# A perceiver's first cross-attention in float16 pairs, keys placed by transfers, transposes among key products, chunks unrolled

## The chip, the cores and the metric

The kernel runs on one core of one Trainium2 chip. The metric is the device time of one execution in microseconds (us), the median of several runs. A core has TensorE (PE; PEld is its weight load), VectorE (DVE), ScalarE (ACT), GpSimd (POOL) and SyncE (SP), which here only issues transfers. The engines run side by side and wait for each other through semaphores. ps is PSUM, the eight accumulation banks.

## The reference

Two perceiver layers on a latent x of 128 x 256 with a context of 12544 x 256: cross-attention, self-attention and a feed-forward part, each behind a layer norm and added to x. Only the first cross-attention is touched:

```python
def _L0_xattn_ref(x, context, ln_gamma, ln_beta, w_q, w_kv, w_out, b_out, gate):
    xn = _layernorm(x, ln_gamma, ln_beta)
    q = (xn @ w_q).reshape(B, SQ, 16, 64)
    k, v = jnp.split(context @ w_kv, 2, axis=-1)        # 12544 x 1024 each
    k = k.reshape(B, SK, 16, 64)
    v = v.reshape(B, SK, 16, 64)
    scores = jnp.einsum('bqhd,bkhd->bhqk', q * 64 ** -0.5, k)
    attn = jax.nn.softmax(scores, axis=-1)
    out = jnp.einsum('bhqk,bkhd->bqhd', attn, v).reshape(B, SQ, 1024)
    return (out @ w_out + b_out) * jnp.tanh(gate[0])
x = x + _L0_xattn_ref(_layernorm(x), ctx_1024, ...)
```

## The kernel before

first_cross_attention walks the context in 14 chunks of 896 keys (CH; 7 tiles of 128) and in each chunk over 16 heads: 224 steps, n = 16 c + h. It is an attention with a running row maximum and a rescaled accumulator. Float32 accuracy is had by splitting each operand into a high and a low part and adding three products (high by high, high by low, low by high); for context, weights, keys and queries the parts are float32r, for values and probabilities float16.

A step n does, by engine and line:

- TensorE: scores of step n+1 (L696, four products of 448 columns: q_hi and q_lo, each over two halves of the keys, into the two banks s_scores; the query of a head is there twice, on partitions 0 to 63 and 64 to 127, and meets the key's high part on one half and its low part on the other); the key product of step n+4 (K_AHEAD; L686, six products of 448, one half of the keys of two heads, into the bank s_k); a value product (L663, six products of 512 columns, one tile of 128 keys by 8 heads, bank s_v) at h = 1 to 7 for this chunk's heads 8 to 15 and at h = 9 to 15 for the next chunk's heads 0 to 7; weighing of step n-1 (L705 to L707, 21 products of 64 or 65 columns); seven float32 transposes of the probabilities (L715).
- ACT: copies the key product out (L440 k_raw) and writes the even head's high half to k_st (L441), then the exponential of step n+1 (L432), v_hi (L424), and the two pT_hi from the transposed banks (L485, L487); decay at every fourth head (L481).
- VectorE: drop at every fourth head (L604), the two pT_lo of step n-1 (L553), the row maximum of the scores n+1 (L545) and neg_max with it (L547), the flush of a group of four heads to acc (L560, L563), c_abs of the next chunk at h = 2 and 4 (L526), v_lo (L538) or, at h = 8, the value scale (L532, L534).
- GpSimd: k_split, three operations of 64 x 448 on float32r, which finish k_st (L363, L367, L370), each behind a semaphore of the one before; at h < 8 one of eight pieces of the next chunk's c_hi and c_lo (L352, L355); the rescaling of acc at every fourth head (L386).
- SP: one load of the next chunk into c_raw per chunk (L324).

k_st holds two head pairs. Each engine runs its list in order. Scores of a step wait for the exponential of the step before, since s_scores is single. Chunks 0 and 1 and chunks 12 and 13 are written out straight; chunks 2 to 11 are a loop of five passes of two chunks, on each engine:

```python
def chunk_pairs(engine, two_chunks):
    two_chunks(0, True, False)
    with engine.Fori(1, NCH // 2 - 1) as i:
        two_chunks(i * 2, False, False)
    two_chunks(NCH - 2, False, True)
```

Before the steps stands a head: layer norm, weight splits, query product and its doubling, the first four key products and the first seven value tiles. The weights of the later ternary feed-forward part are loaded, summed and quantised inside chunks 0, 1, 12 and 13.

## Time and profile before

| | |
|---|---|
| median of 3 runs | 1608.9 us (1608.52 to 1609.34) |
| profiled execution, first to last instruction | 1607.9 us |
| instructions | 30564 |
| busy: PE, PEld | 86%, 71% |
| busy: DVE, ACT, POOL | 66%, 54%, 58% |
| first cross-attention, first to last exponential | 40.0 to 1200.9 us |
| GpSimd's k_split (L363, L367, L370) | 207.3, 250.9, 253.9 us busy |
| row maximum (L545) | 241.7 us busy, 224 times |

The busy share is an average over stages. A row of a group gives the line, the engine, what is written from what with shapes, how often, the busy time, the mean of one instruction, and how long the engine idled before it and for whom. A row of a timeline gives start, duration, engine, line, operation and, in brackets, the idle time before it; "x7" means seven merged. The records of TensorE's products overlap, since they are pipelined: the spacing of their starts is what one costs. "issue" is a wait for nothing that the profile shows.

### The profile page before, as it was taken

The page shows a single profiled execution, that of the slowest core. Times are in us where ns is not written, and L with a number is a line of the kernel's source. Part 1 is how long each engine was busy: PE and PEld are TensorE (multiplying, and loading weights), DVE is VectorE, ACT ScalarE, POOL GpSimd, SP SyncE. Part 2 cuts the span into 40 slices and gives each one's busy share as a digit, 9 for nine tenths or more (in the row PEclk, how much of TensorE's full clock was granted, in tenths as well). Part 3 has the DMA queues.
Part 4 walks back from the last instruction along what each step waited for, and adds up shares of the span by engine and source line. Part 5 has one row for each costly group of instructions (what it writes and reads, how often), then busy time and mean ns, then how long its engine had stood idle before and what let it go on. Part 6 is the DMA issues. An engine that isn't in the chain of part 4 may idle for free. (4 is left out here: it accounts for less than half of the span.)

```text
span 1607.9 us, 30564 instructions
## 1 busy us (share of the span) xinstructions
PE 1379.2 (86%) x10913; PEld 1137.1 (71%) x10913; DVE 1054.0 (66%) x1695; ACT 860.9 (54%) x1614; POOL 926.3 (58%) x850
## 2 busy tenths in 40 slices
PE   5999999998999899989998999999974689515498
PEld 3788888887888788878887788888863348402288
DVE  6677676766777677757676667777753461499732
ACT  4676666665666566656666566678651013154010
POOL 2778777876777686858686778787750000056300
PEclk9999999999999999999999999999997699757789
DMA  6000000000000000000000000000006347030145
GB/s 252 1 24 1 24 1 24 1 24 3 24 2 24 3 24 1 24 3 11 14 4 23 2 24 2 24 1 2 1 27 220 91 166 226 35 151 1 38 178 199
DMA packets 38529, 76.61 MB, mean 48 GB/s; under 512 B 3472, under 2 KB 26832, under 8 KB 38112
## 3 DMA queue, kind: packets, MB, share of 16 engines
q1 hardware_dynamic: 37552, 71.37, 13.1%
q10 hardware_dynamic: 816, 3.15, 0.5%
q8 instruction: 95, 1.56, 0.4%
q14 instruction: 66, 0.54, 0.1%
HBM read 74.34 MB, written 0.16 MB: 46 GB/s over the span
## 5 line engine op out<-in xcount | busy, mean ns | idle before, releaser
L363 POOL TENSOR_TENSOR k_st<-k_raw,one 64x448 fp32r<-64x448 f32 x220 | 207.3, 942 | 248.7 <-ACT k_raw L440 245.9
L538 DVE SCALAR_TENSOR_TENSOR v_lo<-ps,v_scale,v_hi 128x512 f16<-128x512 f32 x196 | 147.0, 751 | 271.9 <-ACT v_hi L424 271.9
L553 DVE TENSOR_TENSOR pT_lo<-ps,pT_hi 128x512 f16<-128x512 f32 x448 | 256.9, 614 | 70.0 <-ACT pT_hi L485 60.4
L432 ACT ACTIVATE p_exp<-ps,neg_max 128x896 f32<-128x896 f32 x224 | 224.7, 1003 | 113.4 <-DVE neg_max L547 112.7
L367 POOL TENSOR_TENSOR k_st<-k_raw,k_st 64x448 fp32r<-64x448 f32 x220 | 250.9, 1141 | 31.5
L440 ACT ACTIVATE k_raw<-ps 128x448 f32<-128x448 f32 x220 | 120.0, 545 | 277.7 <-PE ps L686 277.5
L370 POOL TENSOR_TENSOR k_st<-k_raw,k_st 64x448 fp32r<-64x448 f32 x220 | 253.9, 1154 | 17.3
L545 DVE TENSOR_REDUCE neg_row<-ps 128x1 f32<-128x896 f32 x224 | 241.7, 1079 | 7.1 <-PE ps L696 7.1
L715 PE MATMUL ps<-ident,p_exp 128*128 128x128 f32 x1568 | 217.5, 279 | 0.0
L696 PE MATMUL ps<-k_st,q_hi 128*128 128x448 f32 x448 | 144.6, 404 | 52.8 <-ACT p_exp L432 30.7
L705 PEld LDWEIGHTS ps<-v_hi,pT_hi 128*128 128x128 f16 x1568 | 142.8, 99 | 65.4 <-issue 53.6
L705 PE MATMUL ps<-v_hi,pT_hi 128*128 128x65 f16 x1568 | 169.2, 196 | 5.8 <-DVE pT_lo L553 5.4
L715 PEld LDWEIGHTS ps<-ident,p_exp 128*128 128x128 f32 x1568 | 170.4, 142 | 0.1
L686 PE MATMUL ps<-c_hi,wk_hi 128*128 128x448 f32 x448 | 167.5, 374 | 3.0 <-DVE k_st L588 3.0
L686 PE MATMUL ps<-c_lo,wk_hi 128*128 128x448 f32 x448 | 167.5, 374 | 0.0
L686 PE MATMUL ps<-c_hi,wk_lo 128*128 128x448 f32 x448 | 167.3, 374 | 0.0
L706 PE MATMUL ps<-v_lo,pT_hi 128*128 128x64 f16 x1568 | 167.1, 194 | 0.0
L707 PE MATMUL ps<-v_hi,pT_lo 128*128 128x65 f16 x1568 | 166.3, 194 | 0.0
L663 PE MATMUL ps<-wv_hi,c_hi 128*128 128x512 f32 x392 | 154.4, 394 | 1.0 <-DVE v_lo L538 1.0
L663 PE MATMUL ps<-wv_hi,c_lo 128*128 128x512 f32 x392 | 154.7, 395 | 0.0
L663 PE MATMUL ps<-wv_lo,c_hi 128*128 128x512 f32 x392 | 154.3, 394 | 0.0
L706 PEld LDWEIGHTS ps<-v_lo,pT_hi 128*128 128x128 f16 x1568 | 144.8, 98 | 0.0
(304 smaller groups left out, 2682.0 us busy)
## 6 DMA issues: line engine op xcount, KB each, us to landing
c_raw<-in_ctxT SPq DMA_DIRECT2D x14, 896.0 KB, 4.7
xa_ct<-in_ctxT SPq DMA_DIRECT2D x14, 896.0 KB, 4.7
xa_cn<-in_ctx SPq DMA_DIRECT2D x14, 896.0 KB, 5.2
me_w<-in_me_w SPq DMA_DIRECT2D x8, 1536.0 KB, 7.7
me_w<-in_me_w SPq DMA_DIRECT2D x8, 768.0 KB, 4.7
ss_b_all<-ss_bc SPq DMA_DIRECT2D x1, 2048.0 KB, 6.8
ss_c_all<-ss_bc SPq DMA_DIRECT2D x1, 2048.0 KB, 11.4
wk<-in_wk ACTq DMA_DIRECT2D x1, 1024.0 KB, 5.4
```

What stands on the lines that cost most here:

```text
L363: nc.gpsimd.tensor_tensor(k_st[DH:P, tile, 1, keys], k_raw[DH:P, u % 2, :], one[DH:P, 0, :].to_broadcast([DH, HCH]), ALU.mult).then_inc(k_ ...
L367: nc.gpsimd.tensor_tensor(k_st[DH:P, tile, 0, keys], k_raw[0:DH, u % 2, :], k_st[0:DH, tile, 0, keys].bitcast(F32), ALU.subtract).then_inc ...
L370: nc.gpsimd.tensor_tensor(k_st[0:DH, tile, 1, keys], k_raw[DH:P, u % 2, :], k_st[DH:P, tile, 1, keys].bitcast(F32), ALU.subtract).then_inc ...
L432: nc.scalar.activation(p_exp[:, h % 2, :].rearrange("p (b k) -> p b k", b=2), s_scores, ACT.Exp, bias=neg_max[:, par, h:h + 1]).then_inc(e ...
L545: nc.vector.tensor_reduce(neg_row[:, h % 2:h % 2 + 1], s_scores, AX.XY, ALU.max, negate=True).then_inc(row_max_done, 1)
L553: nc.vector.tensor_tensor(pT_lo[:, h % 2, t0:t1, :], s_t[b][:, 0:(t1 - t0) * S].rearrange("p (t s) -> p t s", s=S), pT_hi[:, h % 2, t0:t1, ...
L663: mm = nc.tensor.matmul(v_bank(use, early), lhs, rhs, start=(k == 0), stop=(k == 5))
L686: mm = nc.tensor.matmul(k_bank(u, early), lhs, rhs, start=(k == 0), stop=(k == 5))
L705: nc.tensor.matmul(s_pv[h // 4 % 2][:, h % 4, :], ph, v_hi[:, tile, h, 0:DH + 1], start=(tile == 0), stop=False)
L706: nc.tensor.matmul(s_pv[h // 4 % 2][:, h % 4, 0:DH], ph, v_lo[:, tile, h, 0:DH], start=False, stop=False)
L707: mm = nc.tensor.matmul(s_pv[h // 4 % 2][:, h % 4, :], pl, v_hi[:, tile, h, 0:DH + 1], start=False, stop=(tile == TILES - 1))
L715: mm = nc.tensor.transpose(s_t[b][:, s * S:(s + 1) * S], p_exp[:, h % 2, tile * P:(tile + 1) * P], ident[:, :])
```

## The change

- All parts are float16. So that they fit, context, weights and query are scaled first: by the largest weight of each input row (w_abs, w_inv) and a bound per chunk (w_bound times c_abs on TensorE, then un, c_scale), the query by q_scale; the exponential takes the inverse as scale (esc), and the new neg_new applies it to the row maximum. v_lo no longer scales and is a tensor_tensor.
- The key product is copied by ACT as before (k_raw), then GpSimd makes k_top (float16 copy, 128 x 448) and k_rest (the remainder), two operations in place of three, and SP places their halves into k_st by four transfers a step. k_st has four pairs, K_AHEAD is 6. The first six key products go by ACT and VectorE.
- TensorE's step: scores n+1, then transposes of step n alternating with the six products of key n+6, then weighing n-1, then the value product, which waits for v_lo of the one before (v_ready).
- VectorE's step: drop, row_max n+1 (three operations), v_lo, first pT_lo, flush, c_abs at h = 2, 3, scale at h = 4, second pT_lo. ACT's step: v_hi, first pT_hi, exponential n+1, second pT_hi, key copy, at h = 6 to 9 c_hi, at every fourth decay.
- GpSimd's step: c_low at h = 7 to 10, c_times at h = 5 to 8 (scaling in place), acc's rescaling at every fourth, k_split.
- No loop; all 14 chunks are written out. The ternary quantisation goes over chunks 2 to 7.

```diff
-K_AHEAD = 4
+K_AHEAD = 6
-        k_st = t("k_st", [P, 2, 2, CH], F32R)
+        k_st = t("k_st", [P, 4, 2, CH], F16)
+        k_top, k_rest = t("k_top", [P, 2, HCH], F16), t("k_rest", [P, 2, HCH], F16)
...
@@ SP @@
+                for n in range(NT):
+                    U = n + K_AHEAD
+                    if U < NT:
+                        b = U % 2
+                        at_least(sp, scores_done, 2 * (U // 2 - 4) + 2)
+                        sp.wait_ge(k_top_ready, U - K_AHEAD + 1)
+                        for side in range(2):
+                            r = DH * side
+                            sp.dma_start(k_st[(slice(r, r + DH),) + k_place(U, side)], k_top[r:r + DH, b, :]).then_inc(k_placed[b], 16)
+                        sp.wait_ge(k_rest_ready, U - K_AHEAD + 1)
+                        for side in range(2):
+                            r, other = DH * side, DH * (1 - side)
+                            sp.dma_start(k_st[(slice(other, other + DH),) + k_place(U, side)], k_rest[r:r + DH, b, :]).then_inc(k_placed[b], 16)
...
@@ GpSimd @@
+                def k_split(U):
+                    i, b = U - K_AHEAD, U % 2
+                    pool.wait_ge(k_raw_ready, i + 1)
+                    if i >= 2:
+                        pool.wait_ge(k_placed[b], k_turn(U - 2))
+                    nc.gpsimd.tensor_copy(k_top[:, b, :], k_raw[:, b, :]).then_inc(k_top_ready, 1)
+                    pool.wait_ge(k_top_ready, i + 1)
+                    nc.gpsimd.tensor_tensor(k_rest[:, b, :], k_raw[:, b, :], k_top[:, b, :], ALU.subtract).then_inc(k_rest_ready, 1)
...
@@ ACT @@
+                for n in range(NT):
+                    c, h = n // H0, n % H0
+                    if n and v_at(n - 1):
+                        v_high(*v_at(n - 1))
+                    at_least(act, pv_done, n - 1)
+                    act.wait_ge(t0_done, n + 1)
+                    turned(n, 0)
+                    if n + 1 < NT:
+                        exponent(n + 1)
+                    act.wait_ge(t1_done, n + 1)
+                    turned(n, 1)
+                    if n + K_AHEAD < NT:
+                        k_copy(n + K_AHEAD)
...
@@ VectorE @@
+                def row_max(n):
+                    v.wait_ge(scores_done, n + 1)
+                    link(nc.vector.tensor_reduce(neg_row[:, i:i + 1], s_scores, AX.XY, ALU.max, negate=True))
+                    link(nc.vector.tensor_scalar(neg_new[:, i:i + 1], neg_row[:, i:i + 1], esc[:, par:par + 1], LN_K, ALU.mult, ALU.add))
+                    nc.vector.tensor_tensor(neg_max[:, par, h:h + 1], neg_new[:, i:i + 1], neg_max[:, 1 - par, h:h + 1],
+                                            ALU.min).then_inc(neg_max_ready, 1)
...
@@ TensorE @@
+                for n in range(NT):
+                    if n + 1 < NT:
+                        scores(n + 1)
...
+                    if U < NT:
+                        k_wait(U)
+                    for tile in range(TILES):
+                        turn(n, tile)
+                        if U < NT and tile < 6:
+                            k_part(U, tile)
...
+                    if n:
+                        weigh(n - 1)
+                    if v_at(n):
+                        v_project(*v_at(n))
```

## Rows read from the trace of the kernel before

**Rows 1.** Windows view, steady stretch: busy us per engine, clock, DMA share, GB/s
```profile
650.00:697.00 47.00, 44.99 (x397) 38.38 (x397) 33.42 (x55) 30.36 (x55) 36.24 (x35) 1.00 0.06 21
```

**Rows 2.** Source view of the exponential's line: durations in ns, first and last start
```profile
L432 ACT ACTIVATE p_exp<-ps,neg_max x224: 992/1007/1011, 40.0 to 1200.9; 128x896 f32<-128x896 f32 x112
```

**Rows 3.** Timeline, ACT, chunk starts: start us, duration, operation, idle before
```profile
797.68 1.01 ACT L432 ACTIVATE p_exp<-ps,neg_max 128x896 f32<-128x896 f32 x1 [0.70 <-DVE neg_max L547]
...
880.18 1.01 ACT L432 ACTIVATE p_exp<-ps,neg_max 128x896 f32<-128x896 f32 x1 [0.70 <-DVE neg_max L547]
...
891.29 0.99 ACT L432 ACTIVATE p_exp<-ps,neg_max 128x896 f32<-128x896 f32 x1
```

**Rows 4.** Timeline, TensorE, at the start of a loop pass
```profile
713.51 0.64 PE L696 MATMUL ps<-k_st,q_hi 128*128 128x448 f32 x2 [2.81 <-issue]
```

**Rows 5.** Timeline of all engines but TensorE's, one step
```profile
652.60 1.01 ACT L432 ACTIVATE p_exp<-ps,neg_max 128x896 f32<-128x896 f32 x1 [0.70 <-DVE neg_max L547]
...
654.22 0.75 DVE L538 SCALAR_TENSOR_TENSOR v_lo<-ps,v_scale,v_hi 128x512 f16<-128x512 f32 x1 [0.66 <-ACT v_hi L424]
...
655.95 1.08 DVE L545 TENSOR_REDUCE neg_row<-ps 128x1 f32<-128x896 f32 x1
...
656.85 0.93 POOL L363 TENSOR_TENSOR k_st<-k_raw,one 64x448 fp32r<-64x448 f32 x1 [0.54 <-ACT k_raw L440]
...
657.07 0.73 DVE L547 SCALAR_TENSOR_TENSOR neg_max<-neg_row,neg_max 128x1 f32<-128x1 f32 x1
...
657.83 1.01 ACT L432 ACTIVATE p_exp<-ps,neg_max 128x896 f32<-128x896 f32 x1 [0.70 <-DVE neg_max L547]
...
657.92 1.14 POOL L367 TENSOR_TENSOR k_st<-k_raw,k_st 64x448 fp32r<-64x448 f32 x1
```

**Rows 6.** Timeline, TensorE, one step
```profile
652.05 0.20 PE L705 MATMUL ps<-v_hi,pT_hi 128*128 128x65 f16 x1
...
652.69 0.96 PE L715 MATMUL ps<-ident,p_exp 128*128 128x128 f32 x7
653.76 0.64 PE L696 MATMUL ps<-k_st,q_hi 128*128 128x448 f32 x2
...
654.64 0.37 PE L686 MATMUL ps<-c_hi,wk_hi 128*128 128x448 f32 x1
...
655.88 0.39 PE L663 MATMUL ps<-wv_hi,c_hi 128*128 128x512 f32 x1
...
657.03 0.40 PE L663 MATMUL ps<-wv_hi,c_lo 128*128 128x512 f32 x1
```

**Rows 7.** Source view of neg_max: minimum, median, maximum in ns
```profile
L547 DVE SCALAR_TENSOR_TENSOR neg_max<-neg_row,neg_max x224: 158/604/942, 39.8 to 1200.7; 128x1 f32<-128x1 f32 x112
```

**Rows 8.** Groups of VectorE by shape, 300 to 1100 us: busy us, mean ns, idle
```profile
L553 DVE TENSOR_TENSOR pT_lo<-ps,pT_hi 128x512 f16<-128x512 f32 x152 | 103.6, 682 | 44.5 <-ACT pT_hi L485 35.0 <-issue 9.5
...
L617 DVE TENSOR_SCALAR wq<-wq 128x1024 f32<-128x1024 f32 x2 | 2.1, 1056 | 0.0
L534 DVE RECIPROCAL v_scale<-v_unscale 128x1 f32<-128x1 f32 x10 | 1.6, 164 | 0.3
```

**Rows 9.** Groups of TensorE's weight loads by shape, up to 1240 us
```profile
L715 PEld LDWEIGHTS ps<-ident,p_exp 128*128 128x128 f32 x1568 | 170.4, 142 | 0.1
...
L705 PEld LDWEIGHTS ps<-v_hi,pT_hi 128*128 128x128 f16 x1568 | 142.8, 99 | 65.4 <-issue 53.6 <-DVE pT_lo L553 9.8 <-DVE acc L563 1.9
```

**Rows 10.** DMA issues up to 60 us: KB each, median us from issue to landing
```profile
c_raw<-in_ctxT SPq DMA_DIRECT2D x2, 896.0 KB, 10.7
...
x<-in_x SPq DMA_DIRECT2D x1, 128.0 KB, 2.8
```

**Rows 11.** Timeline, head: transfer issue, c_abs, score product of step 1
```profile
2.21 0.63 SPq L297 DMA_DIRECT2D rows<-in_rows  x1
...
13.89 2.08 DVE L526 TENSOR_REDUCE c_abs<-c_raw 128x1 f32<-128x896 f32 x2 [0.56 <-DMA c_raw<-in_ctxT]
...
45.33 0.57 PE L696 MATMUL ps<-k_st,q_hi 128*128 128x448 f32 x2
```

More of the change, by code:

```diff
@@ L399, in _, with c_times, c_low @@
-                chunk_pairs(pool, two_chunks)
+                def c_times(c, k):
+                    par = c % 2
+                    pool.wait_ge(c_scale_ready, c + 1)
+                    nc.gpsimd.tensor_scalar(c_raw[raw_part(k)], c_raw[raw_part(k)], c_scale[:, par, k % 2:k % 2 + 1], None,
+                                            ALU.mult).then_inc(c_scaled, 1)
+                def c_low(c, k):
+                    par = c % 2
+                    pool.wait_ge(c_hi_ready, 4 * c + k + 1)
+                    nc.gpsimd.tensor_tensor(c_lo[c_part(par, k)], c_raw[raw_part(k)], c_hi[c_part(par, k)], ALU.subtract).then_inc(c_lo_ready, 1)
@@ new lines, in _ @@
+                for k in range(4):
+                    c_times(0, k)
+                for k in range(4):
+                    c_low(0, k)
+                pool.wait_ge(ones_ready, 5)
+                for n in range(NT):
+                    c, h = n // H0, n % H0
+                    if 7 <= h <= 10 and c + 1 < NCH:
+                        c_low(c + 1, h - 7)
+                    if 5 <= h <= 8 and c + 1 < NCH:
+                        c_times(c + 1, h - 5)
+                    if h % 4 == 3:
+                        g = h // 4
+                        f = c * 4 + g
+                        pool.wait_ge(decay_ready, f + 1)
+                        at_least(pool, flushed, 2 * (f - 3))
+                        grp = acc[:, 4 * g:4 * g + 4, :]
+                        nc.gpsimd.tensor_tensor(grp, grp, decay[:, 4 * g:4 * g + 4].unsqueeze(2).to_broadcast([P, 4, DH + 1]),
+                                                ALU.mult).then_inc(acc_scaled, 1)
+                    if n + K_AHEAD < NT:
+                        k_split(n + K_AHEAD)
@@ new lines, in _, with c_high @@
+                act.wait_ge(w_scale_ready, 2)
+                for c in range(DC):
+                    nc.scalar.activation(wk_hi[:, c, :], wk[:, c, :], ACT.Copy, scale=w_inv[:, c:c + 1]).then_inc(wk_hi_ready, 1)
+                def c_high(c, k):
+                    par = c % 2
+                    act.wait_ge(c_scaled, 4 * c + k + 1)
+                    if c >= 2:
+                        act.wait_ge(k_written, 16 * (c - 1))
+                        act.wait_ge(v_written, 14 * (c - 1))
+                    nc.scalar.activation(c_hi[c_part(par, k)], c_raw[raw_part(k)], ACT.Copy).then_inc(c_hi_ready, 1)
@@ new lines, in _, with v_high @@
+                for k in range(4):
+                    c_high(0, k)
+                act.wait_ge(loaded["wv"], 16)
+                for c in range(DC):
+                    nc.scalar.activation(wv_hi[:, c, :], wv[:, c, :], ACT.Copy, scale=w_inv[:, c:c + 1]).then_inc(wv_hi_ready, 1)
+                def v_high(vn, c, half, tile):
+                    act.wait_ge(v_written, vn + 1)
+                    if tile == 0:
+                        at_least(act, pv_done, c * H0 - (8 if half == 0 else 0))
@@ L690, in scores, with bound, k_wait @@
-                def scores(n, h):
-                    pe.wait_ge(k_ready, n * 2 + (4 if h % 2 == 0 else 2))
+                    mm.then_inc(v_written, 1)
+                def bound(c):
+                    pe.wait_ge(absmax_done, 2 * c + 2)
+                    for d in range(DC):
+                        mm = nc.tensor.matmul(s_bound, w_bound[:, d, :], c_abs[:, c % 2, d:d + 1], start=(d == 0), stop=(d == DC - 1))
+                    mm.then_inc(bound_done, 1)
+                def k_wait(U):
+                    c, u = U // H0, U % H0
+                    if U < K_AHEAD:
+                        at_least(pe, k_early, 2 * (U - 2) + 2)
+                    elif U == K_AHEAD:
+                        pe.wait_ge(k_early, 2 * K_AHEAD)
+                    else:
+                        pe.wait_ge(k_raw_ready, U - K_AHEAD)
+                    if u < 2:
+                        pe.wait_ge(c_lo_ready, 4 * c + 2 + 2 * u)
@@ new lines, in k_part @@
+                def k_part(U, k):
+                    c, u = U // H0, U % H0
+                    d, term, b = k // 3, k % 3, u % 2
+                    m = slice(u // 2 * P, (u // 2 + 1) * P)
+                    keys = slice(b * HCH, (b + 1) * HCH)
+                    lhs = (wk_hi, wk_hi, wk_lo)[term][:, d, m]
+                    rhs = (c_hi, c_lo, c_hi)[term][:, c % 2, d, keys]
+                    mm = nc.tensor.matmul(k_bank(U), lhs, rhs, start=(k == 0), stop=(k == 5))
+                    if k == 5:
+                        mm.then_inc(k_written, 1)
```

677 lines of the change are left out of this document (301 added, 376 removed).

## The prediction

> **What bounds the kernel now.** I read first the windows of the steady stretch of the first cross-attention, then its exponentials in order of time, then all engines inside one step, then the rows that price single instructions. In the window TensorE is busy 45.0 of 47 us, VectorE 33.4, ACT 30.4, GpSimd 36.2 [rows 1], so the stage looks bound by TensorE. It isn't, quite. There is one exponential (L432) per step of chunk and head, 224 of them, from 40.0 to 1200.9 [rows 2]: 1160.9 us of the 1607.9, 5.2 a step. The rest of the kernel I take as untouched. Chunk 9 takes 82.5 us (797.68 to 880.18), but the next interval alone is 11.1 us (880.18 to 891.29) [rows 3]. It opens a pass of the loop, and TensorE stands still there, for 2.8 us at one place, waiting for nothing that the trace shows [rows 4]. Four passes show it, at 5 to 6 us each, 22.8 us in all; the straight chunks 0, 1, 12 and 13 don't.
>
> Inside a pass the cadence is 5.23 us (exponentials at 652.60 and 657.83 [rows 5]), while TensorE needs 0.88 for scores, 1.24 for keys, 1.40 for values, 0.64 for weighing and 0.7 for transposes [rows 6], 4.9 in all. What closes the step is a ring of ACT and VectorE: the exponential ends, v_hi follows on ACT, v_lo on VectorE starts at 654.22, then two pT_lo, the row maximum at 655.95, neg_max at 657.07, the next exponential at 657.83 [rows 5]. In it neg_max, a 128x1 operation, takes 0.73 us and ends when GpSimd's k_st copy ends (656.85 + 0.93 = 657.78 [rows 5]). Over all steps it takes 158 ns at least and 604 at the median [rows 7]: this operation has two SBUF inputs and waits out whatever GpSimd runs.
>
> **The change part by part.** The new order makes other rings. I count from a step's first score product.
>
> *Ring with values (14 of 16 steps).* Four score products: three spacings of 0.19 (below) and one record of 0.37 [rows 6] make 0.94. The row maximum is now first in VectorE's step, no longer behind v_lo and pT_lo: 0.03 + 1.08 [rows 5], to 2.05. Then a new small tensor_scalar. Its bounds are 0.16, VectorE's reciprocal [rows 8], and 0.60, neg_max's median [rows 7]; as it reads one tensor like the reciprocal, I take 0.19 with its semaphore. neg_max at its free 0.16 [rows 7]: 2.45. v_lo, now a plain tensor_tensor from PSUM, costs what pT_lo of that shape does, 0.68 [rows 8]: 3.13. The next value product waits for it (one bank), and with it the next scores, queued behind on TensorE. 0.04, then six products of 512 columns in float16. Spacing today is 0.23 for 512 and 0.207 for 448 columns of float32r, 0.0305 for 65 of float16 [rows 6], which is 2.4 GHz in both with some 19 and 3 ns beside: so 0.217 and 0.19. Six make 1.30, the step **4.45 us**.
>
> *TensorE alone.* Scores 0.76, transposes between key products, weighing 0.64, values 1.30. Now a transpose costs 0.11 ((0.96 - 0.27) / 6 [rows 6]), nearer to its weight load of 0.142 [rows 9] than to its 128 columns at 2.4 GHz (0.055). Beside a key product that load is covered: a pair 0.19 + 0.055, six pairs and one transpose 1.6. With nothing gained it is 6 x 0.30 + 0.11 = 1.9. Weighing ends at 3.0 to 3.3, beside the 3.17 at which v_lo frees the bank: float16 and the alternation save TensorE 0.3 to 0.6 us a step, of which almost nothing is on the ring, and cost it 0.1 at most. Loads that are not covered are a rival.
>
> *Ring without values (heads 0 and 8).* Scores to exponential to scores: 2.45 + 0.04 + 1.01 [rows 5] + 0.15 = **3.65**.
>
> *ACT.* Today 30.4 of 47 us [rows 1], 3.4 a step. The half-wide copy into k_st goes (0.5), c_hi comes (four a chunk, 0.5 each). Both stand behind the key copy, where ACT waits for the next value product; 3.0 of 4.45, hidden.
>
> *VectorE.* 1.08 + 0.19 + 0.16 + 0.68 + 0.68 + 0.55 and some 0.4 for flush, c_abs and scales: 3.7 of 4.45. The last pT_lo ends at 4.6, the next maximum is due at 5.4; without that cover each tenth would be on the ring. The ternary quantisation (1.06 [rows 8] and one more operation in chunks 2 to 7) fits but for some 0.5 us.
>
> *GpSimd.* Three key operations of 0.93, 1.14 and one more like it [rows 5] become a one-input copy and a subtraction of 1.15. The copy's bounds are 0.93, today's two-input form, and half of it; I take 0.6. They start after the previous step's key copy, at 0.1, and end at 1.9 (2.25 by the upper bound), before neg_max at 2.28. So most collisions of today go. They stay where GpSimd's queue is longer: behind acc's rescaling (0.6, heads 0, 4, 8, 12) until 2.75, at heads 5 to 10 for c_times (0.6) and c_low (1.15), both from 1.95, and after each short step. Per chunk 4 x 0.45 + 2 x 0.27 + 4 x 0.8 and some 0.5: 6 us.
>
> *Transfers.* Each step issues four from SP, 56 KB each. An issue takes 0.63 in the row [rows 11], at most 2.5 of SP's 4.45; a load of 128 KB lands 2.8 us after its issue [rows 10]. From key copy to landed keys: 0.6 + 1.15 + 1.2 + 2.8, 5.8 us. k_top's buffer is asked for again after two steps, 8.9 us, the keys after four. Hidden with 3 us to spare. Queued behind the waits on SP is c_raw's load at head 11, needed six heads later.
>
> *Chunk.* 14 x 4.45 + 2 x 3.65 + 6 = **75.6 us** against 82.5. Unrolling takes the 22.8 us of the passes; the straight chunks of today are the evidence. Thirteen chunks make 983, the last (seven steps with values, eight without, 2 of collisions) 62.5: 1045 against 1161, so 116 less.
>
> *Head.* c_raw lands at 13.9, the first score of step 1 leaves at 45.3 [rows 11]. Now scales come first: two maxima of 1.04, two of the 2048-wide weights of 2.4 by the same rate, small ones, to 22; four c_times and four c_low on GpSimd to 29; then on VectorE twelve early key subtractions at 0.6, four q_lo at 0.6 and two wv_lo at 1.2, to 42, and seven value tiles at 1.35, the last of them to 50. That is 5 us more, 12 at worst.
>
> Sum: 1607.9 - 116 + 8 (head 5, 3 for the quantisation, the flush after it and the order at the end) = 1500 as the span. The runs' median is 1.0 above the span: **1501 us**.
>
> **Rivals.** (1) *Collisions in every step.* If the copy takes over 0.93, or the new tensor_scalar waits for GpSimd too, each of the two small operations pays today's median excess (0.60 - 0.16) or less, 0.3: 0.6 a step with values in place of the 6 counted gives 79.5 a chunk, 1501 + 54 = 1555. Against it: the reciprocal took 164 ns in ten of ten beside a busy GpSimd, and a tensor_scalar of 1024 elements 1056 ns, one element a cycle [rows 8]. Of its chance of 0.19, 0.08 is for the tensor_scalar. The Trainium skill (SBUF — State Buffer, "Who interferes with whom") says that tensor_scalar can enter a two-port mode and is then locked out by GpSimd. By that rule this rival is the forecast; the rows on the reciprocal and the 1024-wide operation show neither the mode nor a wait. (2) *No collisions.* The phases settle so that GpSimd is free at each neg_max: 69.6 a chunk, 1501 - 80 = 1420. For it: today's minimum of 158 ns. (3) *Slower: weight loads uncovered.* If each load between a float32 transpose and a float16 product stood alone (0.142 and 0.099 [rows 9]), the pairs would take 7 x 0.2 + 6 x 0.29 = 3.1 and the step 0.76 + 3.1 + 0.64 + 1.30 = 5.8: 1501 + 196 x 1.35 - 20 = 1745. It turns into a loss from 5.0 a step. Against it: loads of 0.099 vanish in spacings of 0.0305 today [rows 6, 9]. (4) *Slower: late landing.* The loop of k_top is (0.93 + 1.15 + 0.3 + 1.2 + L) / 2 a step. With L at 2.8 it is 3.2, it binds from L = 5.3 and passes today's 5.2 from 6.8; the nearest row so long is c_raw's 10.7 in the crowded start [rows 10]. With L at 7.5: some 1650. (5) *It doesn't do what it says* in one part: float16 brings no faster stream, since float32r has 2.4 GHz already; this is in the sum.
>
> **How the numbers follow.** Forecast 0.61 (own range 1455 to 1540), every-step collisions 0.19, none 0.12, uncovered loads 0.04, late landing 0.03, all cancelled to within 0.2% 0.01. A measurement of this kernel can tell about 0.2%, 3 us. Faster 0.92, same 0.01, slower 0.07. The range reaches both collision cases: 1425 to 1562.
>
> **What would show it.** Exponentials 4.45 apart with values, 3.65 without, 75.6 a chunk, none 11 apart. The value product idles until v_lo. neg_max mostly at 0.16, long at heads 4 to 10. Scores never wait for transfers. The copy on GpSimd under 0.93. Step 1 starts at 50. It is wrong if TensorE spaces a pair over 0.3, if transfers land after 5 us, or if VectorE has no gap before the maximum. The granted clock should stay at 1.00, 2.4 GHz, as with 45 of 47 us busy [rows 1].

## The result and the profile after

The changed kernel takes **1469.6 us** (median of 4 runs, 1467.7 to 1470.1) against 1608.7 of the kernel before on the same chip: a ratio of 0.9132, 95% interval 0.9119 to 0.9145, so 139 us less. The forecast was 1501 in a range of 1425 to 1562. The profiled span is 1467.4 us. The page of the profile after, with columns as in [rows 8] (busy us, mean ns, idle time before):

```profile
PE 1273.5 (87%) x10912; PEld 894.1 (61%) x10913; DVE 1039.5 (71%) x1976; ACT 798.2 (54%) x1453; POOL 577.3 (39%) x632
...
L350 POOL TENSOR_TENSOR k_rest<-k_raw,k_top 128x448 f16<-128x448 f32 x218 | 226.1, 1037 | 17.7
...
k_st<-k_top SPq DMA_DIRECT2D x436, 56.0 KB, 2.0
```

GpSimd's share fell from 58% to 39%. Two groups of VectorE stand where [rows 7] stood:

```profile
L534 DVE TENSOR_TENSOR neg_max<-neg_new,neg_max 128x1 f32<-128x1 f32 x224 | 50.1, 224 | 7.6
L533 DVE TENSOR_SCALAR neg_new<-neg_row,esc 128x1 f32<-128x1 f32 x224 | 48.0, 214 | 7.9
```

neg_max now takes 224 ns on average, against a median of 604 [rows 7], and the new small tensor_scalar takes 0.21 us in every one of its 224 records. The answer to [rows 5, 6] is one step in order of time (start, duration, engine, line, and in brackets the idle time before and what ended it):

```profile
694.59 0.54 PE L707 MATMUL ps<-k_st,q_hi 128*128 128x448 f16 x2
...
695.35 0.27 PE L717 MATMUL ps<-ident,p_exp 128*128 128x128 f32 x1
695.46 0.35 PE L693 MATMUL ps<-c_hi,wk_hi 128*128 128x448 f16 x1
...
695.55 1.09 DVE L532 TENSOR_REDUCE neg_row<-ps 128x1 f32<-128x896 f32 x1 [0.94 <-PE ps L707]
695.65 0.27 PE L717 MATMUL ps<-ident,p_exp 128*128 128x128 f32 x1
...
696.92 0.16 DVE L534 TENSOR_TENSOR neg_max<-neg_new,neg_max 128x1 f32<-128x1 f32 x1
697.00 0.68 DVE L525 TENSOR_TENSOR v_lo<-ps,v_hi 128x512 f16<-128x512 f32 x1
...
697.12 1.10 ACT L420 ACTIVATE p_exp<-ps,neg_max,esc 128x896 f32<-128x896 f32 x1
...
697.25 0.19 PE L733 MATMUL ps<-v_hi,pT_hi 128*128 128x65 f16 x1
...
697.88 0.38 PE L665 MATMUL ps<-wv_hi,c_hi 128*128 128x512 f16 x1
...
699.17 0.35 PE L707 MATMUL ps<-k_st,q_hi 128*128 128x448 f16 x1
```

The step lasts 699.17 - 694.59 = 4.58 us, and no TensorE row of it carries a wait. A transpose is followed by its key product 0.11 later, and that by the next transpose 0.19 later: a pair is 0.30. The values start at 697.88, 3.29 into the step, when v_lo has been done for 0.20. The window that answers to [rows 1]:

```profile
640.00:687.00 47.00, 45.98 (x445) 32.41 (x444) 37.09 (x75) 31.68 (x57) 27.67 (x32) 1.00 0.21 51
```

The granted clock is 1.00, 2.4 GHz, as before. The exponentials, in place of [rows 2, 3]: the first two, the first of chunk 9 and the last.

```profile
51.65 1.10 ACT L420 ACTIVATE p_exp<-ps,neg_max,esc 128x896 f32<-128x896 f32 x1 [2.20 <-DVE neg_max L534]
60.73 1.10 ACT L420 ACTIVATE p_exp<-ps,neg_max,esc 128x896 f32<-128x896 f32 x1
...
710.86 1.10 ACT L420 ACTIVATE p_exp<-ps,neg_max,esc 128x896 f32<-128x896 f32 x1
...
1064.58 1.10 ACT L420 ACTIVATE p_exp<-ps,neg_max,esc 128x896 f32<-128x896 f32 x1 [0.48 <-DVE neg_max L534]
```

From first to last it is 1012.9 us, where it was 1160.9. A chunk takes 72.7, its sixteen intervals being 4.58, 3.78, 4.60, 4.57, 4.97, 4.59, 4.58, 4.73, 4.84, 4.01, 4.70, 4.45 and four of 4.58; none stands out as the 11.1 of [rows 3] did. (These intervals run from one exponential to the next. Below, a step runs from its first score product to that of the next step, so a late exponential shows in both neighbours of an interval but in one step.) The first exponential is 11.7 later than before, and the stretch behind the last is 4.2 shorter (402.8 for 407.0), 3.0 of it up to the last flush.

### The profile page after: what moved, and what is told of

Read it like the earlier page. It is cut to its first block and busy times, and to the rows that moved or that the text cites. A ratio compares the mean times of both kernels' runs of the same rounds, so it can differ in the third digit from the quotient of the medians.

```text
span 1467.4 us, 29268 instructions
## 1 busy us (share of the span) xinstructions
PE 1273.5 (87%) x10912; PEld 894.1 (61%) x10913; DVE 1039.5 (71%) x1976; ACT 798.2 (54%) x1453; POOL 577.3 (39%) x632
## 3 DMA queue, kind: packets, MB, share of 16 engines
q10 hardware_dynamic: 816, 3.15, 0.6%
## 5 line engine op out<-in xcount | busy, mean ns | idle before, releaser
L717 PE MATMUL ps<-ident,p_exp 128*128 128x128 f32 x1568 | 423.0, 273 | 1.7 <-ACT p_exp L420 1.4
L431 ACT ACTIVATE pT_hi<-ps 128x512 f16<-128x512 f32 x448 | 241.9, 540 | 260.1 <-PE ps L717 260.1
L420 ACT ACTIVATE p_exp<-ps,neg_max,esc 128x896 f32<-128x896 f32 x224 | 245.7, 1097 | 13.5 <-DVE neg_max L534 8.1
L350 POOL TENSOR_TENSOR k_rest<-k_raw,k_top 128x448 f16<-128x448 f32 x218 | 226.1, 1037 | 17.7
L693 PE MATMUL ps<-c_hi,wk_hi 128*128 128x448 f16 x448 | 158.8, 354 | 5.1 <-POOL c_lo L340 3.7
L693 PE MATMUL ps<-c_hi,wk_lo 128*128 128x448 f16 x448 | 158.8, 354 | 0.0
L693 PE MATMUL ps<-c_lo,wk_hi 128*128 128x448 f16 x448 | 158.8, 354 | 0.0
L733 PEld LDWEIGHTS ps<-v_hi,pT_hi 128*128 128x128 f16 x1568 | 144.1, 97 | 11.1 <-DVE pT_lo L540 0.7
L665 PE MATMUL ps<-wv_hi,c_hi 128*128 128x512 f16 x392 | 148.8, 380 | 2.1 <-DVE v_lo L525 1.3
L665 PE MATMUL ps<-wv_hi,c_lo 128*128 128x512 f16 x392 | 148.5, 379 | 0.0
L665 PE MATMUL ps<-wv_lo,c_hi 128*128 128x512 f16 x392 | 148.5, 379 | 0.0
L707 PE MATMUL ps<-k_st,q_hi 128*128 128x448 f16 x448 | 121.3, 352 | 21.8 <-DMA k_st<-k_top 13.8
```

What stands on the lines that cost most here:

```text
L350: nc.gpsimd.tensor_tensor(k_rest[:, b, :], k_raw[:, b, :], k_top[:, b, :], ALU.subtract).then_inc(k_rest_ready, 1)
L420: nc.scalar.activation(p_exp[:, n % 2, :].rearrange("p (b k) -> p b k", b=2), s_scores, ACT.Exp, bias=neg_max[:, c % 2, h:h + 1], scale=es ...
L431: nc.scalar.activation(pT_hi[:, n % 2, t0:t1, :], s_t[b][:, 0:(t1 - t0) * S].rearrange("p (t s) -> p t s", s=S), ACT.Copy).then_inc(pT_hi_ ...
L665: mm = nc.tensor.matmul(v_bank(vn), lhs, rhs, start=(k == 0), stop=(k == 5))
L693: mm = nc.tensor.matmul(k_bank(U), lhs, rhs, start=(k == 0), stop=(k == 5))
L717: mm = nc.tensor.transpose(s_t[b][:, s * S:(s + 1) * S], p_exp[:, n % 2, tile * P:(tile + 1) * P], ident[:, :])
```

## The experiments

Twelve kernels, in the order of the questions. Unless it says otherwise an edit is made to the changed kernel.

**What is the loop worth?** Only the unrolling, in the kernel before:

```diff
-    with engine.Fori(1, NCH // 2 - 1) as i:
+    for i in range(1, NCH // 2 - 1):
         two_chunks(i * 2, False, False)
```

> The kernel before, with its five loop passes written out and nothing else changed. Theory: the four intervals of 10 to 11 us at pass starts go, 22.8 us, 1609 to 1586. Rival: straight code of this length waits for its instructions too, the time stays within 5 us of 1609.

Measured: 1569.8 us, ratio 0.9762 (0.9745 to 0.9779), 38 less. The passes' starts gave their 22.8; most of the rest came from inside the passes. Three exponentials round the middle of a chunk of this kernel:

```profile
808.40 1.01 ACT L432 ACTIVATE p_exp<-ps,neg_max 128x896 f32<-128x896 f32 x1 [0.71 <-DVE neg_max L547]
813.54 1.01 ACT L432 ACTIVATE p_exp<-ps,neg_max 128x896 f32<-128x896 f32 x1 [0.71 <-DVE neg_max L547]
818.20 1.01 ACT L432 ACTIVATE p_exp<-ps,neg_max 128x896 f32<-128x896 f32 x1 [0.22 <-DVE neg_max L547]
```

A step with values is 5.15 here and 5.23 in the loop [rows 5], the one after it 4.65 (5.43 in the loop), the chunk 80.9 for 82.5. The missing 16 are 13 inside the ten chunks of the loop and 3.0 in chunks 12 and 13, which are straight in both kernels. The 5.43 is not the loop itself: in the chunks that open a pass the same step takes 4.66. It turns on which operation starts first. In chunk 9 neg_max starts at 843.25, just behind GpSimd's L363 at 843.24, and takes 0.94 us; in chunk 10 it starts at 932.10, ahead of L363 at 932.25, and takes 0.16. Why the other steps take 0.08 less stays open. So of the 139 us, 38 are the unrolling and 101 the rest, if the unrolling is worth as much in the changed kernel; the changed kernel with a loop was not run.

**What bounds the step: TensorE or the ring through v_lo?** First the products back in float32r, with the order as it is:

```diff
-        wk_hi, wk_lo = t("wk_hi", [P, DC, INNER], F16), t("wk_lo", [P, DC, INNER], F16)
+        wk_hi, wk_lo = t("wk_hi", [P, DC, INNER], F32R), t("wk_lo", [P, DC, INNER], F32R)
...
-        c_hi, c_lo = t("c_hi", [P, 2, DC, CH], F16), t("c_lo", [P, 2, DC, CH], F16)
+        c_hi, c_lo = t("c_hi", [P, 2, DC, CH], F32R), t("c_lo", [P, 2, DC, CH], F32R)
```

(wv_hi and wv_lo likewise)

> The changed kernel with context and weights of the key and value products as float32r pairs again, the rest left. Theory: TensorE closes the step, each of twelve products costs 0.017 to 0.02 us more, 0.2 to 0.24 a step with values and half without: 43 to 50 us, 1515. Rival, the ring as predicted: only the six value products are on it and 0.15 us of room stand before them, under 10 us more, 1478.

Measured: 1520.7, ratio 0.9458 (0.9442 to 0.9474), 51 more. The step with values is 4.87 to 4.89, 0.30 more: 0.10 in the six pairs (0.315 each) and 0.18 in the six value products. All that TensorE needs more shows in the step, so TensorE bounds it. v_lo still ends at 3.10 and the values start at 3.39, so the ring has more room than before; the rival, in which the ring covered a part, fell.

Then the transposes cheaper. The probabilities are rounded to float32r before they are turned, and so lose their lowest bits:

```diff
-        p_exp = t("p_exp", [P, 2, CH])
+        p_exp, ident_r = t("p_exp", [P, 2, CH], F32R), t("ident_r", [P, P], F32R)
...
-                    mm = nc.tensor.transpose(s_t[b][:, s * S:(s + 1) * S], p_exp[:, n % 2, tile * P:(tile + 1) * P], ident[:, :])
+                    mm = nc.tensor.transpose(s_t[b][:, s * S:(s + 1) * S].bitcast(F32R), p_exp[:, n % 2, tile * P:(tile + 1) * P], ident_r[:, :])
```

> The changed kernel with probabilities and identity of the transposes as float32r (the probabilities lose their lowest bits). Theory: a float32 transpose is bound by its streaming at half rate, 0.11 us; as float32r it takes 0.055 to 0.06, TensorE's step falls from 4.58 to 4.2, and then the ring of row maximum and v_lo closes the step at 4.43: 1440. Rival 1: the weight load of a 32-bit operand is the bound, float32r costs the same 0.11, time stays at 1469. Rival 2: no ring behind TensorE, the step falls the whole 0.4: 1390.

Measured: **1451.1**, ratio 0.9021 (0.9006 to 0.9037), faster than both kernels. Its pairs:

```profile
780.09 0.38 PE L720 MATMUL ps<-ident_r,p_exp 128*128 128x128 f32 x1
780.32 0.36 PE L696 MATMUL ps<-c_hi,wk_hi 128*128 128x448 f16 x1
780.36 0.38 PE L720 MATMUL ps<-ident_r,p_exp 128*128 128x128 f32 x1
```

0.27 a pair where float32 has 0.30. The values start at 3.15, 0.05 behind v_lo: the ring is reached, and the step is 4.45, which is what the prediction had for it. 1440 had been expected. In chunk 10 most steps gave 0.12, heads 1, 4 and 9 gave 0.22, heads 0 and 8 nothing, and heads 7 and 10 grew by 0.12 and 0.22: there neg_max stands under c_lo, which now starts later in the step, and TensorE no longer hides the wait. Both fixed costs of the expectation fell: a float32r transpose comes neither at 0.055 nor at 0.11.

**Is the alternation worth anything?** All seven transposes, then the six key products:

```diff
                     for tile in range(TILES):
                         turn(n, tile)
-                        if U < NT and tile < 6:
-                            k_part(U, tile)
+                    for k in range(6):
+                        if U < NT:
+                            k_part(U, k)
```

> The changed kernel with the seven transposes in one block ahead of the six key products. Theory from the changed kernel's trace: a transpose takes 0.11 us of TensorE wherever it stands, the alternation hides nothing, so the time stays within 3 us of 1469.6. Rival, the step as predicted: a key product covers half of a transpose, so 0.3 us a step come back, some 60 us, 1530.

Measured: 1469.1, ratio 0.9133 (0.9117 to 0.9149), the same as with alternation. A float32 transpose costs TensorE 0.11 beside a key product and 0.11 beside another transpose. In the run with `bound` at head 0 and float32r transposes in a block, below, those start 0.086 apart.

**What is the row maximum's place worth?**

```diff
-                    if n + 1 < NT:
-                        row_max(n + 1)
                     if n and v_at(n - 1):
                         v_low(*v_at(n - 1))
+                    if n + 1 < NT:
+                        row_max(n + 1)
```

> The changed kernel with v_lo ahead of the row maximum on VectorE. Theory: TensorE closes the step at 4.58 and the ring over v_lo has 0.15 us of room, so taking v_lo off it saves only heads 7 and 10, 0.2 us a chunk: 0 to 4 us less, 1467. Rival, the ring as predicted: the step is closed by v_lo, 0.15 us or more a step, 25 us less.

Measured: 1530.3, ratio 0.9515 (0.9488 to 0.9541), 61 more: both expectations were wrong. The step at head 8 of chunk 10, whose first score product is at 873.24:

```profile
873.88 0.58 ACT L400 ACTIVATE c_hi<-c_raw 128x448 f16<-128x448 f32 x1
874.35 0.21 ACT L474 ACTIVATE decay<-drop 128x4 f32<-128x4 f32 x1
874.44 0.60 ACT L413 ACTIVATE v_hi<-ps 128x512 f16<-128x512 f32 x1
...
875.08 0.69 DVE L525 TENSOR_TENSOR v_lo<-ps,v_hi 128x512 f16<-128x512 f32 x1 [0.92 <-ACT v_hi L413]
875.68 1.08 DVE L532 TENSOR_REDUCE neg_row<-ps 128x1 f32<-128x896 f32 x1
```

v_lo waits for v_hi, and v_hi stands in ACT's queue behind the key copy, c_hi and decay. Where these are few the order costs nothing (4.58 still, although v_lo is off the ring); at head 8 the maximum starts 2.4 into the step instead of 0.95, and neg_max, now at another place of the step, runs into GpSimd for 0.83 (heads 7, 8 and 0 together cost 2.9 a chunk). About 25 of the 61 stand in chunks 0 to 7, at heads 9 and 11 to 13, where chunks 9 to 12 lose nothing; what holds the steps there was not followed. I had followed v_lo on VectorE and not the queue of the engine that feeds it.

**Who holds neg_max?** A GpSimd operation is added after k_rest in six of sixteen steps, once with two SBUF inputs, once with one:

```diff
+                    if i % H0 in (1, 2, 3, 13, 14, 15):
+                        link(nc.gpsimd.tensor_tensor(spare[:, 1, :], spare[:, 0, :], spare[:, 0, :], ALU.subtract))
```

> The changed kernel with an idle operation of two inputs, 128x896, some 2 us, on GpSimd behind k_rest in six steps of a chunk, so that it lies over neg_max. Theory: neg_max (two SBUF inputs) waits for its end, from 0.16 to about 1.4 us, v_lo and the value product behind it, some 0.95 us in six steps of 14 chunks: 80 us, 1550. Rival: the 0.15 us of room and other slack take it, under 15 us.

Measured: 1509.7, ratio 0.938 (0.936 to 0.940), 40 more. The one-input kind has tensor_scalar with a pointer operand, 640 wide, in the same place:

```diff
+                        link(nc.gpsimd.tensor_scalar(spare[:, 1, 0:640], spare[:, 0, 0:640], one[:, 0:1], None, ALU.mult))
```

> The same place and about the same length (2 us), but one tensor input: tensor_scalar of 640 elements. Theory from c_times (L334), which lies over neg_max at heads 5 and 6 while neg_max takes 0.16: a one-input operation on GpSimd doesn't hold neg_max, time within 3 us of 1469.6. Rival: any GpSimd operation that reads SBUF holds it, 80 us more as with two inputs.

Measured: 1471.2, ratio 0.9139 (0.9119 to 0.9159), no effect. The added operation and neg_max, first with two inputs, then with one:

```profile
L353 POOL TENSOR_TENSOR spare<-spare 128x896 f32<-128x896 f32 x81 | 136.0, 1679 | 0.0
L537 DVE TENSOR_TENSOR neg_max<-neg_new,neg_max 128x1 f32<-128x1 f32 x224 | 95.8, 427 | 7.6
```

```profile
L353 POOL TENSOR_SCALAR spare<-spare,one 128x640 f32<-128x640 f32 x81 | 152.6, 1884 | 0.0
L537 DVE TENSOR_TENSOR neg_max<-neg_new,neg_max 128x1 f32<-128x1 f32 x224 | 50.5, 225 | 7.6
```

Under the two-input operation 54 neg_max take 0.88 to 1.10, to its end. Under the one-input one, which is longer, 54 take 0.16, and the mean stays at 225. That looks as if one input didn't hold neg_max at all, but these 54 all start 0.65 us or more into the added operation, and the 26 of neg_max under c_times in the changed kernel start 0.75 into it. An earlier start stands in the run with v_lo first, at head 7 of chunk 10:

```profile
871.41 1.40 POOL L334 TENSOR_SCALAR c_raw<-c_raw,c_scale 128x448 f32<-128x448 f32 x1
...
871.62 0.43 DVE L534 TENSOR_TENSOR neg_max<-neg_new,neg_max 128x1 f32<-128x1 f32 x1
```

neg_max starts 0.21 into c_times and ends 0.64 into it. Over all runs 16 records start 0.20 to 0.48 into a c_times, and every one ends at 0.64 or 0.65; the 310 that start 0.50 or later take their free 0.16. So c_times holds neg_max for the first 0.64 of its 1.40 us and then lets it go, while a two-input operation holds it to the end. The experiment above did not test that early part. One record starts under GpSimd's cast k_top (at 76.97 in the run with a block and `bound` at head 0, below); it was held, 0.41, to the cast's end.

With two inputs four of the six steps grew, to 5.3 or 5.4; in the other two, behind the rescaling of acc, the operation started after neg_max. That is why 40 came and not 80.

**Can the remaining collisions be ordered away?** c_times, one input, goes ahead of c_low, two inputs:

```diff
+                    if 6 <= h <= 9 and c + 1 < NCH:
+                        c_times(c + 1, h - 6)
                     if 7 <= h <= 10 and c + 1 < NCH:
                         c_low(c + 1, h - 7)
-                    if 5 <= h <= 8 and c + 1 < NCH:
-                        c_times(c + 1, h - 5)
```

> Only GpSimd's order changes: c_times at heads 6 to 9 instead of 5 to 8, and ahead of c_low in each step. Theory (only a GpSimd operation with two SBUF inputs holds neg_max): the one-input c_times takes the stretch from 1.6 to 3.0 us of the step, over neg_max, and c_low starts behind neg_max, at 3.0. So neg_max falls to 0.16 at heads 7, 8 and 9, stays long at head 10 where c_low stands alone, and the 1.0 us a chunk of collisions shrinks to 0.2 to 0.4: 13 x 0.7 = 9 less, 1461 (1457 to 1465). Rival (any GpSimd operation that reads SBUF holds it): c_times, longer than c_low, holds neg_max at four heads until 3.0, 0.7 late, 3 us a chunk instead of 1: 1495.

Measured: 1471.3, ratio 0.9138 (0.9123 to 0.9153), no gain. Head 10 of chunk 10, in the changed kernel and then in this one:

```profile
832.45 1.04 POOL L340 TENSOR_TENSOR c_lo<-c_raw,c_hi 128x448 f16<-128x448 f32 x1
...
833.02 0.49 DVE L534 TENSOR_TENSOR neg_max<-neg_new,neg_max 128x1 f32<-128x1 f32 x1
```

```profile
834.56 1.04 POOL L340 TENSOR_TENSOR c_lo<-c_raw,c_hi 128x448 f16<-128x448 f32 x1
...
834.82 0.80 DVE L534 TENSOR_TENSOR neg_max<-neg_new,neg_max 128x1 f32<-128x1 f32 x1
```

neg_max ends when c_lo ends, within 0.02 (833.51 and 833.49; 835.62 and 835.60). The theory held at head 7 (neg_max fell from 0.31 to 0.16). At heads 8 and 9 it had the wrong operation: in both kernels neg_max there ends with k_rest, which comes late behind the rescaling and the short step, and not with c_lo (head 9: 0.41 and 0.40; head 8: 0.55 and 0.42). At head 10 the longer queue pushed c_lo back, and the collision grew by 0.31. In step time heads 7 and 8 gave 0.03 and 0.13, head 10 took 0.31, and the chunk went from 72.7 to 72.9. The rival's 1495 fell: c_times lies over neg_max 26 times here, at 0.16 each, since each time it had started 0.72 us or more before.

**Why is head 4 longer?** The two float32 products of L672 (`bound`), which the prediction left out, stand there. They are moved to head 0, a step without values:

```diff
-                    if h == 4 and c + 1 < NCH:
+                    if h == (4 if c == 0 else 0) and c + 1 < NCH:
                         bound(c + 1)
```

(from chunk 1 on also: c_abs of chunk c+2 at heads 14 and 15, the scale at head 0, and another bank)

> The two float32 products `bound` move from head 4, a step with values, to head 0, one without (from chunk 1 on), with the maxima of the next context chunk at heads 14 and 15 of the chunk before and the scales at head 0. Theory: a step with values is bound by TensorE, so head 4 loses its 0.4 us; a step without values is bound by the exponential's ring, with TensorE idle 0.4 or more, so head 0 gains nothing: 12 x 0.4 = 5 less, 1465 (1463 to 1467). Rival: head 4's 0.4 us is not `bound` but the wait for what VectorE has queued at heads 2 to 4 (maxima, scales), and then the time moves with them to heads 14 to 0: 1470 to 1474.

Measured: 1470.7, ratio 0.9133 (0.9117 to 0.9148), no gain. Head 4 did fall from 4.98 to 4.58, and head 0 rose from 3.77 to 4.15. ACT at head 0 of chunk 10, first in the changed kernel (first score product at 785.63), then here (786.45):

```profile
787.65 0.60 ACT L431 ACTIVATE pT_hi<-ps 128x512 f16<-128x512 f32 x1 [1.22 <-PE ps L717]
788.16 1.10 ACT L420 ACTIVATE p_exp<-ps,neg_max,esc 128x896 f32<-128x896 f32 x1
```

```profile
788.87 0.60 ACT L431 ACTIVATE pT_hi<-ps 128x512 f16<-128x512 f32 x1 [1.62 <-PE ps L720]
789.37 1.09 ACT L420 ACTIVATE p_exp<-ps,neg_max,esc 128x896 f32<-128x896 f32 x1
```

neg_max ends at 2.49 of the step in both. The exponential starts at 2.53 there and at 2.92 here, because the first pT_hi stands ahead of it on ACT and waits for the fourth transpose, which `bound` has put back. Neither the theory nor the rival had this: the exponential has two gates, neg_max and ACT's queue, and in the changed kernel they open within 0.1 of each other. At head 4 of the changed kernel the same gate had put the exponential at 2.91.

The three moves together:

> The changed kernel with transposes in float32r (probabilities rounded to that type before they are turned), GpSimd's c_times ahead of c_low, and `bound` at head 0. If the three savings add: 1451 - 9 - 5 = 1437. With the transposes shortened the step with values is bound by VectorE's ring as much as by TensorE, so moving `bound` may give nothing (1442), while a late neg_max costs more than before, so the order of c_low may give up to 12 (1434). Range 1432 to 1444.

Measured: 1451.3, ratio 0.9016 (0.9000 to 0.9032), what the float32r transposes give alone, and above the expected range. Beside that kernel the intervals of chunk 10 show each move giving and taking alike: 0.24 less at head 4 and 0.24 more at head 0 for `bound`, 0.28 less at head 7 and 0.30 more at head 10 for c_times. Then what the theory of the second gate asks for, transposes in a block so that pT_hi comes early, with `bound` at head 0:

> The changed kernel with float32r transposes, all seven of them in a block ahead of the six key products, and `bound` at head 0 from chunk 1 on. Theory: ACT's queue made e11 gain nothing. The exponential of the next head stands there behind the first pT_hi copy, which waits for the fourth transpose; where `bound` comes first that copy ends at 3.02 us of the step instead of 2.62, and the exponential at head 0 starts at 2.92 instead of 2.53. With the transposes in a block the first pT_hi ends before neg_max even behind `bound`, the exponential stays at 2.53, the step at head 0 at 3.77, and head 4 falls to that of its neighbours, 4.45: 12 x 0.3 = 4 us less than float32r alone (1451.1), 1447 (1445 to 1449.5). Rival: the step without values is bound by TensorE too once `bound` is in it (0.76 + 0.4 + 2.4 + 0.6), so head 0 stays over 4.0 and the time at 1451.

(e11 is the run with `bound` at head 0 alone.)

Measured: 1451.3 (1448.7 to 1452.5), ratio 0.9025 (0.9013 to 0.9038). The mechanism is right, the time isn't. Head 0 of chunk 10 (first score product at 771.08):

```profile
772.82 0.60 ACT L434 ACTIVATE pT_hi<-ps 128x512 f16<-128x512 f32 x1 [0.94 <-PE ps L723]
773.61 1.10 ACT L423 ACTIVATE p_exp<-ps,neg_max,esc 128x896 fp32r<-128x896 f32 x1 [0.19 <-DVE neg_max L537]
```

pT_hi is done first, the exponential waits for neg_max and starts at 2.53; head 0 stays 3.77 with `bound` in it and head 4 falls to 4.45. Chunks 9 to 12 take 71.0 for 71.3. But in chunks 3 to 8 the step at head 0 is 4.22 and the chunk 71.5: at head 15 VectorE now has c_abs and a ternary operation, ends its last pT_lo at 10.20 instead of 9.21 (counted from head 14's first score) and starts the maximum 0.25 late. That is half of the 0.44. The other half is GpSimd's. The ternary operation of VectorE starts just ahead of GpSimd's rescaling of acc (chunk 5, first score product at 414.12):

```profile
414.27 0.68 DVE L643 TENSOR_SCALAR tf_up<-wv 128x1024 bf16<-128x1024 f32 x1
414.28 1.15 POOL L372 TENSOR_TENSOR acc<-acc,decay 128x260 f32<-128x260 f32 x1 [2.88 <-ACT decay L477]
...
416.70 0.36 DVE L537 TENSOR_TENSOR neg_max<-neg_new,neg_max 128x1 f32<-128x1 f32 x1
```

The rescaling takes 1.15 there instead of 0.62, in these six chunks and in no other, k_rest ends at 2.92 instead of 2.40, and neg_max pays 0.20. So chunks 1, 2 and 9 to 12 gained 0.2 to 0.3, chunks 0 and 3 to 8 lost 0.1 to 0.2, and from first to last exponential 0.3 us remain.

**What hides the transfers?**

```diff
-K_AHEAD = 6
+K_AHEAD = 4
```

> The changed kernel with K_AHEAD 4 in place of 6. Theory: keys land 10.1 us after the start of the step that makes them (copy 4.5, GpSimd 1.7, transfers 3.9); six ahead leaves four steps, 18.3 us, four ahead leaves two, 9.2. So the scores of even steps wait and two steps take the 10.1 us: 5.05 a step, 90 to 105 us more, 1565. Rival: landing is quicker than it looks, same time within 5 us.

Measured: 1553.5, ratio 0.9659 (0.9628 to 0.9689), 84 more (six less than expected at least).

```profile
L707 PE MATMUL ps<-k_st,q_hi 128*128 128x448 f16 x448 | 122.3, 355 | 80.9 <-DMA k_st<-k_rest 59.5 <-issue 13.5 <-DMA k_st<-k_top 4.3
```

Scores wait 80.9 us in all, mostly for the keys' transfers; in the changed kernel it is 21.8. They don't wait at every second step, as the theory had it, but mostly at heads 0, 8, 9 and 12, which take 1.4, 1.6, 1.1 and 0.7 more. Heads 0 and 8 are the short steps, which leave the transfers the least time; the wait at head 12 was not followed. Each transfer lands in 2.0 in both. The path that GpSimd had walked in place is now copy, split, issue, landing, and only the distance of six steps covers it.

## Why the prediction was right, and where its steps were not

The span was forecast at 1500 and is 1467.4. First to last exponential is 32.1 under the forecast (1012.9 for 1045), the first exponential 6.7 over, the end 7.2 under: 32.6 in all. That the time came so near is partly luck. The forecast had some 70 us too much for collisions, and against them some 32 too little for TensorE, `bound` and the short steps, and 11 too little up to the second exponential. What ran is nearer to rival 2, almost no collisions, than to the 6 us a chunk of the forecast. By its own steps:

- **Ring with values, 4.45.** The ring was sized right: v_lo ends at 3.10 where 3.13 stood, and with float32r transposes the step is 4.45 (the prediction's own terms, 3.13 + 0.04 + 1.30, add up to 4.47). But the end was set by TensorE, at 4.58; the value product never idles for v_lo, which "what would show it" had asked for. "Beside a key product that load is covered" was the step that failed; a pair takes 0.30, the case called "nothing gained", and weighing ends at 3.29. The prediction had kept this to 0.1 and it is 0.13, 1.8 a chunk.
- **Ring without values, 3.65.** 3.77, the exponential at 1.10 instead of 1.01; it now takes its scale from a tile (esc), which was not tried alone. Its second gate, pT_hi ahead of it on ACT, wasn't seen; it opened at the same moment.
- **Collisions, 6 us a chunk.** The term most off: 0.62. k_rest ends at 1.6, not 1.9 (1.04 for 1.15), and behind acc's rescaling at 2.27, just before neg_max starts at 2.33, where 2.75 had been counted (four times 0.45). What is left shows in step time only at heads 7, 8 and 10: 0.03, 0.39 and 0.20. At head 7 the 0.13 that TensorE has over the ring takes up nearly all of it, and at head 9 no v_lo hangs on neg_max: its step is 4.61, like that of head 1, where neg_max is free. "Waits out whatever GpSimd runs" was too wide: c_times at heads 5 and 6 lies over neg_max, which still takes its free 0.16 because it starts 0.75 into it. The prediction had no such case, and here it is luck: up to 0.48 into it neg_max would have waited.
- **`bound`.** Left out; 0.40 a chunk.
- **Chunk.** 75.6 + 1.8 + 0.2 - 5.4 + 0.4 + 0.06 (heads 1 and 9, 0.03 each) = 72.7, as measured. Over twelve chunks the forecast was 34.5 too long.
- **The loop.** 22.8 was read off the passes' starts; undoing it alone gave 38. The sum was built from steps and didn't use it, but the share given to the rest was too large by 15.
- **GpSimd and transfers.** The copy at 0.57 (0.6), a landing at 2.0 (2.8), scores that hardly wait: right. c_times at 1.40, or 1.68 in the head, was priced at 0.6; the nearest row was the copy's, and whether the pointer operand is what costs was not tried.
- **Head, 5 us.** It is 12.3 at the second exponential. Step 1's scores leave at 58.2, not 50:

```profile
22.99 6.70 POOL L334 TENSOR_SCALAR c_raw<-c_raw,c_scale 128x448 f32<-128x448 f32 x4 [20.09 <-DVE c_scale L516]
29.65 4.01 POOL L340 TENSOR_TENSOR c_lo<-c_raw,c_hi 128x448 f16<-128x448 f32 x4
...
34.90 1.28 DVE L585 TENSOR_TENSOR k_st<-ps,k_st 64x448 f16<-64x448 f32 x2 [3.52 <-ACT k_st L443]
...
58.19 0.55 PE L707 MATMUL ps<-k_st,q_hi 128*128 128x448 f16 x2 [1.42 <-DVE v_lo L525]
```

  The scales are ready at 22.9 (22 forecast). c_times takes 6.7 instead of 2.4; VectorE's early subtractions start at 34.9, not 29. From there come 13.7 us, where the prediction had 13, and 9.5 for the value tiles: its own 7 x 1.35, of which its end at 50 had left only 8.
- **The end.** 3 more was forecast for the quantisation, the flush and the order at the end. The quantisation costs nothing that shows (chunks 2 to 7 take 72.7 like 9 to 12), and the end is 4.2 less, 3.0 of it because the last flush comes sooner after the last exponential. I hadn't read those rows. In them the granted clock is 0.50, 1.2 GHz, before (1203.6 to 1206.6 us), behind a wait of TensorE of 2.3 us, and 1.00, 2.4 GHz, after (1065.7 to 1069.1), where the waits are 1.4, 0.3 and 0.55 us; the 21 weighings take 1.1 us before and 0.65 after. How much of the 3.0 is the clock and how much the order was not separated.
- **The rivals.** (1) Every-step collisions fell twice over: the copy is short, and the new tensor_scalar took 0.21 in 69 records that lie wholly under a two-input GpSimd operation. Its price was added up wrongly: 0.6 in 14 steps in place of 6 gives 78.0 a chunk and some 1534, not 79.5 and 1555. (2) No collisions is what nearly came: 0.62 a chunk, though neg_max is free of GpSimd in only 129 of 224. Its 1420 missed because its 69.6 a chunk lacks the same 1.8, 0.2 and 0.4. (3) Between float32 transposes and float16 products TensorE pays 0.05 a pair over the forecast, not 0.25. That it is the weight load isn't shown: float32r transposes in a block start 0.086 apart with loads as long (0.14). (4) Late landing didn't come, but four steps ahead instead of six would have cost 84.

One reading of the prediction was plainly wrong, though its conclusion on the small operation held. It took the 1056 ns of the 1024-wide tensor_scalar [rows 8] as one element a cycle. It was the mean of two kinds. In the kernel before:

```profile
1081.20 1.14 POOL L367 TENSOR_TENSOR k_st<-k_raw,k_st 64x448 fp32r<-64x448 f32 x1
...
1081.46 1.43 DVE L617 TENSOR_SCALAR wq<-wq 128x1024 f32<-128x1024 f32 x1
...
1086.15 0.68 DVE L617 TENSOR_SCALAR wq<-wq 128x1024 f32<-128x1024 f32 x1
...
1086.35 1.47 POOL L367 TENSOR_TENSOR k_st<-k_raw,k_st 64x448 fp32r<-64x448 f32 x1
```

The one that starts inside a GpSimd operation ends 0.55 after it; the one that starts first takes 0.68, and GpSimd's operation is then 1.47 instead of 1.14. The rescaling of acc above, at 1.15 instead of 0.62, is the same. After the change all twelve such operations take 0.68 or 0.69. The Trainium skill (SBUF — State Buffer, "Who interferes with whom") says that tensor_scalar has a two-port mode and that whoever issues first holds the shared pair; these rows agree. It also says that a VectorE operation with two SBUF inputs contends with a GpSimd instruction that reads SBUF. For two-input GpSimd operations the runs agree. For GpSimd's one-input tensor_scalar they agree for the first 0.64 of 1.40 us and not for the rest (310 of 310 neg_max at 0.16), and there the measurement decides.

One wait of the profile after is put down to the wrong cause. Behind the step of head 8 the scores wait 0.7 us, and the profile names the transfer k_st<-k_top. It is the exponential: in all thirteen chunks those scores start 0.145 us after its end, as they do behind head 0, while the nearest landing is 0.4 us or more earlier in twelve of them.

What stays open: why a transpose in float32 costs 0.11 wherever it stands and one in float32r 0.086 in a block, why a step of the loop costs 0.08 more, and what c_times does after 0.64 us that lets neg_max go.

## What to carry to other kernels

An operation's start has as many gates as there are things queued before it: follow the queue of the engine that feeds it, not only its own inputs, and before moving work into a step that "has room", ask what it pushes back in each queue. An operation added as a test tests only the overlap that it makes: look at where in it the other one starts. A mean from a grouped view can be two kinds of record; look at single rows before it becomes a rate. When two limits lie within 0.1 us of each other, removing one gives only their distance, as the float32r transposes (0.13 a step) and the moved `bound` (nothing) showed.
